# A four-layer convolution pipeline on one core: clips of the up-sampled image in pairs, and the second block's normalised image in the padded buffer

## What is computed

```
x = x + conv3x3(relu(n * mask(n))) + bias        # layer 0, n = groupnorm(x)
x = x + down(clip(leaky(up(n + bias)) ...))      # layer 1, n = groupnorm(x)
x = x + state_space_block(n)                     # layer 2, n = groupnorm(x)
x = x + down(clip(leaky(up(n + bias)) ...))      # layer 3, n = groupnorm(x)
```

## Time and profile before

| | |
|---|---|
| median of 3 runs | 6166.72 us |
| lowest and highest | 6165.22 and 6172.53 us |
| the profiled execution's own time | 6170.05 us |
| its span (first to last instruction) | 6168.2 us |
| mean granted TensorE clock | 0.965 |
| busy: PE, DVE, ACT, POOL | 5670.2, 5789.3, 4072.5, 127.8 us |
| clips L1113 | x1152, 445.4 us busy |
| scans L1242 | x704, 2336.6 us busy |

### The profile page before, as it was taken

How to read it: one execution, slowest core, us unless ns; L and a number is a source line. 1 busy time by engine, 2 the same in 40 slices (tenths; PEclk the granted TensorE clock), 3 DMA queues, 4 the chain that set the end, 5 groups by cost and what they waited for, 6 DMA issues and landing times.

```text
span 6168.2 us, 87368 instructions
## 1 busy us (share of the span) xinstructions
PE 5670.2 (92%) x32332; PEld 3724.0 (60%) x32332; DVE 5789.3 (94%) x4684; ACT 4072.5 (66%) x7971; POOL 127.8 (2%) x69
## 2 busy tenths in 40 slices
...
GB/s 55 104 95 94 110 88 96 111 92 98 113 90 96 110 98 92 112 83 102 112 86 100 107 83 108 107 86 106 102 89 109 107 87 105 101 88 111 109 78 52
DMA packets 332404, 597.08 MB, mean 97 GB/s; under 512 B 105206, under 2 KB 174014, under 8 KB 331850
## 3 DMA queue, kind: packets, MB, share of 16 engines
...
## 4 chain that ended last, share of the span: by engine, by line
DVE 43%; PE 18%; issue 17%; ACT 15%; SPq 4%; DMA 2%; DVEq 0%; ACTq 0%
DVE hb L1242 17%; DVE hb L1257 8%; PE ps L639 4%; DVE hb L1225 4%; PE ps L675 3%; DVE ys L1113 3%; PE ps L658 2%; SPq L510 2%; PE ps L619 2%; DVE hb L1220 2%; PE ps L751 2%; ACT xp L858 2%; ACT da L1012 2%; ACT da L1007 2%; SPq L494 2%
## 5 line engine op out<-in xcount | busy, mean ns | idle before, releaser
L1242 DVE TENSOR_TENSOR_SCAN hb<-da,hb 128x1570 f32<-128x1570 f32 (+2 forms) x704 | 2336.6, 3345 | 91.7 <-ACT da L1012 90.2
L604 PE MATMUL ps<-pad,conv_w 128*128 128x392 f32 x4608 | 1577.3, 495 | 0.0
L604 PEld LDWEIGHTS ps<-pad,conv_w 128*128 128x128 f32 x4608 | 862.9, 189 | 635.6 <-issue 24.1
L658 PEld LDWEIGHTS ps<-down_k,ys 121*128 121x128 f32 x9216 | 1108.5, 192 | 153.3 <-issue 65.6
L639 PE MATMUL ps<-xt,up_k 123*121 123x256 f32 (+2 forms) x4096 | 1132.2, 415 | 27.1 <-ACT ys L898 19.1
L1257 DVE TENSOR_TENSOR hb<-hb,c_t 128x3136 f32<-128x3136 f32 (+1 forms) x384 | 1150.3, 3009 | 3.4
L658 PE MATMUL ps<-down_k,ys 121*128 121x121 f32 (+1 forms) x9216 | 1135.2, 274 | 0.4 <-DVE xb L1177 0.3
L1012 ACT ACTIVATE da<-delta_t,a_neg 128x784 f32<-128x784 f32 x1024 | 908.2, 945 | 170.7 <-DVE hb L1242 168.8
L898 ACT ACTIVATE ys<-ps 121x512 f32<-121x512 f32 x1152 | 659.4, 591 | 406.5 <-PE ps L639 271.5
L1225 DVE TENSOR_TENSOR hb<-dx_t,b_t 128x3136 f32<-128x3136 f32 x256 | 869.6, 3419 | 1.4
L639 PEld LDWEIGHTS ps<-xt,up_k 123*121 123x121 f32 x4096 | 639.8, 184 | 307.5 <-ACT ys L898 109.9
...
## 6 DMA issues: line engine op xcount, KB each, us to landing
b_t<-scr SPq DMA_DIRECT2D x256, 392.0 KB, 4.7
dx_t<-vc SPq DMA_DIRECT2D x256, 392.0 KB, 6.6
delta_t<-vd SPq DMA_DIRECT2D x256, 392.0 KB, 6.9
c_t<-scr SPq DMA_DIRECT2D x256, 392.0 KB, 4.0
...
```

Source lines behind the costliest of these rows:

```text
L604: mm = nc.tensor.matmul(ps[:, half, 0:HALF], conv_w[:, c, tap, m * P:(m + 1) * P], pad[:, c, r0:r0 + HH // 2, tap % 3:tap % 3 + WW], start ...
L658: mm = nc.tensor.matmul(img(ps[:, reg, 0:17 * WW])[:, h + h0:h + h1, w + w0:w + w1], ys[0:KP, y % NY, at + n * P:at + (n + 1) * P], down_k ...
L1242: nc.vector.tensor_tensor_scan(h, a, b, 0.0, ALU.mult, ALU.add).then_inc(scan_done, 1)
```

## The change

- `clip` takes one or two steps of ys at a time, by the table CLIPS: in the first image half (0,1), (2,3), (4,5), (6,7), 8; in the second 0, (1,2), (3,4), (5,6), (7,8). It waits for the last of its leaky steps and then counts up_clipped up by one or two. The number of elements clipped is the same.
- Layer 2's gp, gv and gn write into pad instead of xp, behind this sample's convolution, and in_proj reads pad. The next sample's first statistics step in pad waits for f1 and z. The norms of the other layers no longer wait for them.
- conv_w is loaded in two halves on a semaphore of its own, s_conv, which PE awaits ahead of the first convolution.
- All tables but POOL_ORDER are written anew.

```diff
+CLIPS = [[(0, 2), (2, 4), (4, 6), (6, 8), (8, 9)], [(0, 1), (1, 3), (3, 5), (5, 7), (7, 9)]]
...
 PE_ORDER = """
-cen.2@2 yi.3@2 gm1.3@1 var.2@2 gm2.3@1 f1@1 z@1 red.8@2 f2@1 gm2.1@3 f3@1 bc.0@1 red.9@2 turn.0.0.0@3 turn.0.0.1@3
+turn.0.0.1@3 turn.0.0.2@3 f1@1 red.8@2 turn.0.0.3@3 turn.0.1.0@3 z@1 up.0.0.0@3 up.0.0.1@3 f2@1 up.0.0.2@3 up.0.0.3@3
...
-        g2 = xp[:, :, :, :].rearrange("p c j n -> p (c j n)")[:, 0:NC * HW].rearrange("p (c n) -> p c n", c=NC)
...
+        s_conv = sem("s_conv")
...
-            (conv_b[:, :], t["conv_b"]), (neg_mw[:, :], t["mask_w"]), (filt[:, :], t["filt"]), (conv_w[:, :, :, :], t["conv_w"]),
+            (conv_b[:, :], t["conv_b"]), (neg_mw[:, :], t["mask_w"]), (filt[:, :], t["filt"]),
...
+                for c in range(NC):
+                    sp.dma_start(conv_w[:, c, :, :], t["conv_w"][:, c, :, :]).then_inc(s_conv, 16)
...
+                    if s == 0 and g == 0 and n == 0:
+                        pe.wait_ge(s_conv, 16 * NC)
...
-                                                  g2[:, c, half * HALF:(half + 1) * HALF], start=(c == 0), stop=(c == 1))
+                                                  pad[:, c, 1 + half * (HH // 2):1 + (half + 1) * (HH // 2), 1:WW + 1], start=(c == 0), stop=(c == 1))
...
-                    if k == CONV_GN:
+                    if k in (CONV_GN, B_GN):
                         return inner(c)
-                    if k == B_GN:
-                        return img(g2[:, c, :])
...
-                            act.wait_ge(conv_sum, 4 * s)
+                            act.wait_ge(slot_full, max(full("f1", s - 1), full("z", s - 1)))
                         else:
                             act.wait_ge(s_zero, 1)
                     elif k == B_GN:
-
-                        act.wait_ge(turned, 4 * chunk_pass(FIRST, s, 1) + 4)
+                        act.wait_ge(conv_sum, 4 * (s + 1))
...
-                        if k == LAST_GN or s in (1, 2):
-
-                            n = min(s + 2, N_SAMPLES - 1) if k == LAST_GN else s - 1
-                            act.wait_ge(slot_full, max(full("f1", n), full("z", n)))
...
-                def clip(s, p, c, u):
-                    y = N_UP * chunk_pass(p, s, c) + u
-                    v = ys[0:KP, y % NY, :]
+                def clip(s, p, c, j):
+
+                    u0, u1 = CLIPS[c][j]
+                    y = N_UP * chunk_pass(p, s, c) + u0
+                    v = ys[0:KP, y % NY:y % NY + u1 - u0, :]
...
-                    dve.wait_ge(up_leaky, y + 1)
-                    nc.vector.tensor_scalar(v, v, CLAMP, -CLAMP, ALU.min, ALU.max).then_inc(up_clipped, 1)
+                    dve.wait_ge(up_leaky, y + u1 - u0)
+                    nc.vector.tensor_scalar(v, v, CLAMP, -CLAMP, ALU.min, ALU.max).then_inc(up_clipped, u1 - u0)
```

More of the change, by code:

```diff
@@ L81 @@
 SP_ORDER = """
-cl.7@2 bl.8@2 spill@1 load@0 bl.9@2 bcw.0@1 bcw.1@1 cl.8@2 cl.9@2 cl.0@1 bcw.2@1 bl.0@1 xl.0.2@1 dl.0.2@1 bl.1@1
-dl.1.3@1 xl.1.3@1 cl.1@1 store@3 back@2 bl.2@1 xl.2.2@1 xl.2.3@1 dl.2.3@1 xl.2.0@1 xl.2.1@1 dl.2.0@1 dl.2.2@1 bl.3@1
-dl.2.1@1 cl.3@1 cl.2@1 bl.4@1 cl.4@1 bl.5@1 bl.7@1 bl.6@1 cl.5@1 xl.3.2@1 xl.3.1@1 xl.3.0@1 xl.3.3@1 dl.3.1@1 dl.3.0@1
-dl.3.2@1 dl.3.3@1 cl.6@1
+dl.3.2@2 dl.3.3@2 cl.6@2 spill@1 bl.8@2 bl.9@2 cl.7@2 load@0 bcw.0@1 bcw.1@1 bcw.2@1 cl.8@2 bl.0@1 cl.9@2 xl.0.2@1
@@ L86 @@
+dl.0.2@1 cl.0@1 bl.1@1 cl.1@1 dl.1.3@1 xl.1.3@1 store@3 back@2 xl.2.0@1 dl.2.1@1 dl.2.0@1 dl.2.3@1 xl.2.3@1 dl.2.2@1
+xl.2.1@1 bl.2@1 xl.2.2@1 bl.3@1 bl.4@1 bl.5@1 cl.2@1 cl.3@1 cl.5@1 bl.6@1 bl.7@1 cl.4@1 xl.3.3@1 xl.3.0@1 xl.3.1@1
+xl.3.2@1 dl.3.0@1 dl.3.1@1
 """
 PE_ORDER = """
-cen.2@2 yi.3@2 gm1.3@1 var.2@2 gm2.3@1 f1@1 z@1 red.8@2 f2@1 gm2.1@3 f3@1 bc.0@1 red.9@2 turn.0.0.0@3 turn.0.0.1@3
-bc.1@1 turn.0.0.2@3 turn.0.0.3@3 bc.2@1 turn.0.1.0@3 up.0.0.0@3 up.0.0.1@3 up.0.0.2@3 v.0@1 up.0.0.3@3 up.0.0.4@3
@@ L101 @@
-turn.1.1.2@0 down.1.0.5@0 down.1.0.6@0 turn.1.1.3@0 down.1.0.7@0 up.1.1.0@0 up.1.1.1@0 down.1.0.8@0 up.1.1.2@0
-up.1.1.3@0 red.6@1 up.1.1.4@0 up.1.1.5@0 down.1.1.0@0 down.1.1.1@0 down.1.1.2@0 down.1.1.3@0 up.1.1.6@0 up.1.1.7@0
-down.1.1.4@0 up.1.1.8@0 red.7@1 down.1.1.5@0 down.1.1.6@0 down.1.1.7@0 down.1.1.8@0
+turn.0.0.1@3 turn.0.0.2@3 f1@1 red.8@2 turn.0.0.3@3 turn.0.1.0@3 z@1 up.0.0.0@3 up.0.0.1@3 f2@1 up.0.0.2@3 up.0.0.3@3
+f3@1 gm1.0@0 red.9@2 bc.0@1 up.0.0.4@3 bc.1@1 up.0.0.5@3 down.0.0.0@3 down.0.0.1@3 down.0.0.2@3 down.0.0.3@3 bc.2@1
@@ new lines @@
+up.0.0.6@3 up.0.0.7@3 down.0.0.4@3 up.0.0.8@3 turn.0.1.1@3 down.0.0.5@3 turn.0.1.2@3 turn.0.1.3@3 down.0.0.6@3 v.0@1
+up.0.1.0@3 up.0.1.1@3 down.0.0.7@3 gm2.0@0 down.0.0.8@3 up.0.1.2@3 up.0.1.3@3 up.0.1.4@3 up.0.1.5@3 down.0.1.0@3
+down.0.1.1@3 down.0.1.2@3 up.0.1.6@3 v.1@1 red.10@2 up.0.1.7@3 up.0.1.8@3 red.11@2 down.0.1.3@3 down.0.1.4@3 yi.0@1
+cen.3@2 down.0.1.5@3 down.0.1.6@3 var.3@2 down.0.1.7@3 down.0.1.8@3 yi.1@1 v.2@1 conv.0.0@0 conv.0.1@0 conv.0.2@0
+conv.0.3@0 conv.0.4@0 red.0@1 red.1@1 conv.0.5@0 conv.1.0@0 bo.0@2 conv.1.1@0 bo.1@2 conv.1.2@0 conv.1.3@0 conv.1.4@0
@@ new lines @@
+cen.0@1 conv.1.5@0 gm1.1@2 var.0@1 conv.2.0@0 conv.2.1@0 red.2@1 conv.2.2@0 red.3@1 conv.2.3@0 conv.2.4@0 cen.1@1
+conv.2.5@0 conv.3.0@0 conv.3.1@0 conv.3.2@0 conv.3.3@0 conv.3.4@0 conv.3.5@0 var.1@1 gm1.2@0 yi.2@1 red.4@1 gm2.2@0
+v.3@1 red.5@1 turn.1.0.0@0 turn.1.0.1@0 turn.1.0.2@0 turn.1.0.3@0 turn.1.1.0@0 turn.1.1.1@0 up.1.0.0@0 up.1.0.1@0
+up.1.0.2@0 up.1.0.3@0 down.1.0.0@0 down.1.0.1@0 up.1.0.4@0 up.1.0.5@0 down.1.0.2@0 down.1.0.3@0 up.1.0.6@0 up.1.0.7@0
+down.1.0.4@0 turn.1.1.2@0 turn.1.1.3@0 down.1.0.5@0 up.1.0.8@0 down.1.0.6@0 down.1.0.7@0 up.1.1.0@0 down.1.0.8@0
```

60 lines of the change are left out of this document (26 added, 34 removed).

## The result

The changed kernel takes **6137.39 us** (median of 5 runs, 6132.86 to 6142.05) against 6166.72 before: ratio 0.9949, 95% interval 0.9938 to 0.9961. That is 29 us or 0.5% faster. The forecast was 6095 us, 72 us faster: the sign is right, the size more than twice too large. The profiled execution of the changed kernel took 6133.45 us, with a span of 6131.7.

What follows compares the result with a forecast made beforehand. VectorE, 94% busy, was taken to set the pace, with TensorE close behind. Terms of -35 - 72 + 15 + 14 + 12 - 7 = -73 us gave 6097, set at 6095 us against the median; range 6050 to 6145 us.

Steps and rivals of the forecast that it cites:

- Merges, 35 us: Clips of image halves on VectorE: 512 merges in the run, each giving back 0.068 us, 35 us less.
- the row of clips in a row: Three successive VectorE clips, one started every 0.333 us, from which the price of a merge, 0.068 us, was taken.
- Waits for da, 72 us: VectorE's scans waiting for ScalarE's decay factors: skip product and transposes fill TensorE's gap before f1, saving 2.4 us per period.
- Both waits that the forecast named: VectorE's waits at two scans for decay factors, 2.29 us and 1.47 us (0.9 in the mean), both expected to go.
- A new wait at the mask: Smallest branch's last softplus step, spreads and Square: VectorE waits 1.7 us, distances cost 0.6 more; 15 us more in the run.
- they shift by the same and have slack: Rest of the next branch's softplus, mask and convolution, queued behind L1183: delayed equally, with slack to take it.
- Two leaky steps, +14 us: Paired clip awaiting its second leaky step, 0.2 us, and a softplus step 0.3 us before the Square is done; 14 us more.
- Dependent small steps, +12 us: Small VectorE steps formerly separated by clips: four more dependent neighbours, 0.4 us per period, 12 us more.
- Start, 7 us: Filling at the start: statistics no longer await the convolution's weights, so it starts 6.6 us sooner, 7 us less.
- The period: One sample's time between image spills, taken as 186.8 us from four periods and expected to become 184.5 us.
- five rivals: Clock low before f1 (0.20), waits only move (0.12), whole fixed part saved (0.07), four-tile ring binds (0.07), slow wide clip (0.02).
- The clock stays low ahead of f1: Rival, chance 0.20: TensorE's clock stays low at f1's product, so 44 us saved in place of 72; 6123 us.

Runs made afterwards that it cites:

- early chain: Changed kernel with the smallest branch's softplus steps sp2 to sp4 ahead of the two products with C: 6007.67 us; with each paired clip split in two, 6061.95 us.
- the filled gap: Unread matmuls in TensorE's idle time: seven ahead of f1's product in the kernel before, 6126.79 us; five ahead of the variance product in the changed kernel, 6080.5 us.
- the transposes taken away: Changed kernel with sp2 to sp4 early, and two transposes and their copies moved from ahead of f1's product and copy to behind them: 6058.33 us.

## Why the prediction was half right

*Merges, 35 us.* Right as DVE's work, by the runs with the early chain: 34.0 us. Wrong as a term of a sum: worth 54 us where DVE sets the pace, and about nothing (7 us, not certain) in the changed kernel, where DVE waits for PE. The rule of the Trainium skill, page "VectorE: DVE Perf Modes", section "The TRN2 errata — SBUF-src ops pay a fixed extra latency per instruction", would have made it an estimated 80 us; by these runs the pitch of 0.333 us, from the row of clips in a row, was the better guide.

*Waits for da, 72 us.* The mechanism is shown by two runs, the filled gap (41.5 us) and the transposes taken away (51 us), and by the rows of f1's product. In the changed kernel da's waits fell by 44.0 us in 24 periods, 1.8 each, 57 us. It was mis-sized by a fifth. Both waits that the forecast named are gone. What is left is a third, at the scan ahead of them, 0.32 us before and 0.94 now, which the forecast didn't look at. Before, and then in the change:

```profile
3263.08 3.43 DVE L1242 TENSOR_TENSOR_SCAN hb<-da,hb 128x1570 f32<-128x1570 f32 x1 [0.32 <-ACT da L1012]
```
```profile
2325.18 2.73 PE L734 MATMUL ps<-f,dvd 128*128 128x392 f32 x4
...
2328.07 0.26 ACT L838 ACTIVATE rstd<-ps,cst 128x2 f32<-128x2 f32 x1 [0.84 <-PE ps L593]
```

Its da stands on ACT behind layer 2's norm, and the norm waits for the second statistics product (L593), which in the change stands on PE behind the skip product. That took 2.73 us and not the forecast's 1.3, and the norm starts 8.3 us after the spill in place of 7.1. This is read from the rows, not tried.

***The step that failed: "A new wait at the mask", +15 us,*** and in it the sentence on the work queued behind L1183: "they shift by the same and have slack". The chain is late, as forecast. DVE's own wait was even smaller, 0.9 us a period in place of 1.7, and with the distances' 0.4 it is less than what DVE waited there before (1.8). But I followed the chain on DVE alone. Behind the same Square stand ACT's centring copy and, through it, the variance product in PE's queue, and behind L1183 on DVE the clip that the last down steps need; PE idles 2.0 us and more. DVE's waits for PE that follow, put at nothing, are 31.2 + 11.5 us in 24 periods, 1.8 us each or 55 us in the run. PE had only 10.6 us of slack in 180, as the forecast noted itself under the rivals, and behind the gap its clock falls in 23 of 28 periods. Shown: the late chain costs 130 us in all (early chain), of which the filled gap gives back 57 without moving anything. That is the clock's part. The other 73 us I put down to the chain itself: with the gap filled the period is 183.17 us against 180.90, and DVE still waits 22.4 us for the Square, 11.6 for the down steps and 9.3 for the distances in 24 periods, 1.8 us of the 2.3. That division is read from the trace, not tried.

*Two leaky steps, +14 us.* Not so: clips waited 0.6 us in 24 periods where they had waited 8.5. The Square that the softplus step waits for there was in time.

*Dependent small steps, +12 us.* Neither shown nor refuted; no run isolates it. By its own rows a dependent neighbour costs 0.04 + 0.09 = 0.13 us, four of them 0.5 us a period and 16 us in the run. DVE's work fell by 21.9 us in the changed kernel and by 43.2 with the early chain, with the same instructions as there, so more than the merges moves it, and by more than this term.

*Start, 7 us.* Right: 6.7 us at the first spill (129.33 to 122.65); 4.7 us at the end in the kernel with the early chain. The 8.1 us behind the last spill stand in no term of the forecast, and no run isolates them.

*The period.* Four periods weren't enough in a kernel whose periods differ by 4 us: 186.8 for 185.75.

None of the five rivals described what happened. That the time lies within the stated range is luck: the range reached so far up for a clock that stays low ahead of f1, and there it was full. "The clock stays low ahead of f1" had the right cause at the wrong place.
